# Hash experts' down projection as three half-precision products, and the engines' order lists searched anew

## The reference

```python
x = x + _L0_attn_ref(_layernorm(x), L0_attn_Wqkv, L0_attn_Wo)
x = x + _L0_xattn_ref(_layernorm(x), ctx_2048)
x = x + _L0_ffn_ref(_layernorm(x), ...)               # 16 routed experts and a shared one
x = x + _L1_attn_ref(_layernorm(x), ...)              # ternary weights
x = x + _L1_xattn_ref(_layernorm(x), tokens, ctx_2048, ctx_2048, ctx_2048)
x = x + _L1_ffn_ref(_layernorm(x), ...)               # ternary weights

# _L1_xattn_ref
for e in range(4):
    g = silu(einsum('bsd,fd->bsf', hidden, Wg[e]))
    u = einsum('bsd,fd->bsf', hidden, Wu[e])
    y = einsum('bsf,df->bsd', g * u, Wd[e])
    out = where(expert_ids == e, y, out)
```

## Time and profile before

| | before |
|---|---|
| median of 3 runs | 535.25 us (533.11 to 536.31) |
| profiled execution: device time | 534.2 us |
| profiled execution: span | 532.4 us |
| TensorE busy | 493.6 us, 93% |
| VectorE busy | 396.9 us, 75% |
| ScalarE busy | 345.2 us, 65% |
| GpSimd busy | 190.4 us, 36% |

### The profile page before, as it was taken

How to read it: one execution, slowest core, us unless ns; L and a number is a source line. 1 busy time by engine, 2 the same in 40 slices (tenths; PEclk the granted TensorE clock), 3 DMA queues, 4 the chain that set the end, 5 groups by cost and what they waited for, 6 DMA issues and landing times.

```text
span 532.4 us, 11834 instructions
## 1 busy us (share of the span) xinstructions
PE 493.6 (93%) x4694; PEld 362.3 (68%) x4721; DVE 396.9 (75%) x917; ACT 345.2 (65%) x601; POOL 190.4 (36%) x288
## 2 busy tenths in 40 slices
PE   5869887899999999999999999999999999999985
PEld 3424533567778788877887878777777676678654
DVE  2787997879677988548996587644876568689984
ACT  5666744766676236894269845588535874976796
POOL 3129986741340150330004072613052221032562
PEclk9987999899999999999999999999999999999999
DMA  8502443220000001000000020200000300000001
GB/s 290 216 0 63 149 162 114 71 81 1 1 3 1 2 10 71 1 2 2 1 1 2 1 80 3 81 1 1 1 1 2 120 1 1 1 2 2 0 27 55
DMA packets 5943, 21.66 MB, mean 41 GB/s; under 512 B 896, under 2 KB 3072, under 8 KB 5120
## 3 DMA queue, kind: packets, MB, share of 16 engines
q1 hardware_dynamic: 5888, 20.91, 11.6%
HBM read 19.86 MB, written 1.05 MB: 39 GB/s over the span
## 4 chain that ended last, share of the span: by engine, by line
PE 67%; DVE 16%; ACT 9%; issue 4%; POOL 3%; DMA 1%; ACTq 0%; DVEq 0%; POOLq 0%
PE ps L1072 24%; PE ps L1106 15%; PE ps L820 4%; DVE nmx L2524 3%; PE ps L951 3%; PE ps L844 2%; PE ps L880 2%; PE ps L1082 2%; PE ps L928 2%; PE ps L875 2%; PE ps L798 2%; PE ps L970 1%; PE ps L931 1%; DVE hl L2642 1%; PE ps L1152 1%
## 5 line engine op out<-in xcount | busy, mean ns | idle before, releaser
L2631 DVE TENSOR_TENSOR hs<-hs,ps 128x512 f32<-128x512 f32 (+1 forms) x68 | 45.2, 668 | 40.0 <-PE ps L1072 27.3
L1952 ACT ACTIVATE hs<-ps 128x512 f32<-128x512 f32 (+1 forms) x68 | 39.4, 581 | 51.1 <-PE ps L1072 42.7
L2524 DVE TENSOR_REDUCE nmx<-ps 128x2 f32<-128x512 f32 (+1 forms) x96 | 60.4, 681 | 7.2 <-PE ps L880 7.1
L556 POOL TENSOR_TENSOR ve<-mv,half 128x2 f32<-128x2 f32 x24 | 7.7, 322 | 149.0 <-DVE mv L2418 149.0
L1106 PE MATMUL ps<-w2h,hh 128*128 128x256 f16 x200 | 54.7, 274 | 0.7 <-DVE hl L2642 0.5
L1106 PE MATMUL ps<-w2h,hl 128*128 128x256 f16 x200 | 54.6, 273 | 0.0
L1106 PE MATMUL ps<-w2l,hh 128*128 128x256 f16 x200 | 54.6, 273 | 0.0
L1959 ACT ACTIVATE hh<-hs 128x512 f16<-128x512 f32 (+1 forms) x52 | 31.5, 611 | 34.5 <-DVE hs L2637 23.3
L2642 DVE TENSOR_TENSOR hl<-hs,hh 128x512 f16<-128x512 f32 (+1 forms) x52 | 40.1, 779 | 8.9 <-ACT hh L1959 8.6
L1911 ACT ACTIVATE pk<-ps 128x512 f32<-128x512 f32 x64 | 34.6, 597 | 12.1 <-PE ps L931 9.6
L1072 PE MATMUL ps<-yah,w1h 128*128 128x256 f16 x200 | 38.4, 274 | 1.9 <-DVE hs L2631 1.9
(11 more groups left out here) (249 smaller groups left out, 1338.5 us busy)
## 6 DMA issues: line engine op xcount, KB each, us to landing
stage<-in_w SPq DMA_DIRECT2D x12, 800.0 KB, 4.3
tstage<-in_tern SPq DMA_DIRECT2D x4, 1024.0 KB, 4.9
cs<-in_ctxT SPq DMA_DIRECT2D x1, 1024.0 KB, 9.4
cd<-in_ctxT SPq DMA_DIRECT2D x1, 1024.0 KB, 4.8
out_x<-xs SPq DMA_DIRECT2D x4, 256.0 KB, 2.2
sels<-in_sel SPq DMA_DIRECT2D x1, 800.0 KB, 9.8
w0s<-in_w SPq DMA_DIRECT2D x1, 768.0 KB, 7.0
xs<-in_x SPq DMA_DIRECT2D x1, 768.0 KB, 8.2
```

The lines of the kernel that those rows point to most:

```text
L1952: act.activation(hs[:, n % 3, 0:w], ps[:, gate_bank(n), 0:w], ACT.Silu).then_inc(e_sil.sem, 1)
L2524: dve.tensor_reduce(nmx[:, int(n % 3 > 0), first + par:first + 2 * heads:2], ps[:, max_bank(it, n) + par, :].rearrange("p (h k) -> p h k", ...
L2631: TT(hs[:, n % 3, 0:w], hs[:, n % 3, 0:w], ps[:, up_bank(n), 0:w], ALU.mult).then_inc(e_hb.sem, 1)
```

## The change

The hash pairs go the way of the mixture pairs: `inner_high` and `inner_low` for n = 52 to 67 too, and `down(n)` with `hh`, `hl` and the context's halves `ch` and `cl`. The fp32 tile `cd`, its DMA of 1 MB and its semaphore are gone. All four lists have a new order, and the numbers of `awake` matmuls are new (135 in `awake` calls of the list instead of 110).

```diff
-            sp.dma_start(cd[:, :, :, :], ctxT).then_inc(d_cd.sem, 16)
             def down(n):
                 kind, b, p = pair_of(n)
                 last = tiles_of(n) - 1
+                pe.wait_ge(e_lo.sem, n + 1)
                 if kind == "moe":
-                    pe.wait_ge(e_lo.sem, n + 1)
                     if p == 0 and b:
                         pe.wait_ge(xm_ok.sem, b)
                     bank, first, final = 1, p == 0, n + 1 == pairs_upto(kind, b)
-                    terms = [(hh[:, n % 2], w2h), (hh[:, n % 2], w2l), (hl[:, n % 2], w2h)]
+                    high, low = [t[:, 2 * p * D:2 * (p + 1) * D].rearrange("p (k d) -> p k d", d=D)
+                                 for t in (w2h, w2l)] if last else \
+                                [t[:, 2 * p * D:(2 * p + 1) * D].rearrange("p (k d) -> p k d", d=D) for t in (w2h, w2l)]
                 else:
-                    pe.wait_ge(e_hb.sem, n + 1)
-                    if n == ALL_MOE:
-                        pe.wait_ge(d_cd.sem, 16)
                     bank, first, final = gate_bank(n), True, True
-                    terms = [(hs[:, n % 3], None)]
+                    high, low = ch[:, p, :, :], cl[:, p, :, :]
+                terms = [(hh[:, n % 2], high), (hh[:, n % 2], low), (hl[:, n % 2], high)]
...
             def silu_of(n):
                 act.wait_ge(e_a.sem, n + 1)
                 if n >= 3:
-                    act.wait_ge(e_lo.sem if n - 3 < ALL_MOE else e_dn.sem, n - 2)
+                    act.wait_ge(e_lo.sem, n - 2)
...
             def inner_high(n):
-                act.wait_ge(e_hc.sem, n + 1)
+                act.wait_ge(e_hc.sem if n < ALL_MOE else e_hb.sem, n + 1)
```

Of the lists, the places that are spoken of below. GpSimd, start:

```diff
             split_lo(0)
-            context_split()
             split_lo(1)
             split_lo(2)
             split_lo(3)
             split_lo(4)
+            context_split()
+            rsqrt_ln('context', 0)
             split_lo(5)
-            rsqrt_ln('context', 0)
```

TensorE, start (`awake` after this: 30 up to `gate(0)` instead of 49):

```diff
             scores_max(0, 5)
+            awake(6, 3)
             project(1, 0)
+            awake(3, 14)
             maxima_turned(0)
             scores_exp(0, 0)
+            project(1, 1)
             scores_exp(0, 1)
-            project(1, 1)
...
-            awake(7, 10)
+            awake(7, 21)
             maxima_turned(1)
```

More of the change, by code:

```diff
@@ L724, in _ @@
             limited(4, 2)
+            rsqrt_ln('router', 3)
+            ternary(1)
             low_parts(5, 0)
             low_parts(5, 1)
-            ternary(1)
             limited(4, 3)
@@ L731, in _ @@
             ternary(2)
-            rsqrt_ln('tail', 0)
             limited(5, 0)
             limited(5, 1)
+            rsqrt_ln('tail', 0)
             rsqrt_ln('head', 6)
@@ L1350, in _ @@
             context_products(1)
+            scores_exp(2, 2)
             up(3)
@@ L1541, in _ @@
+            up(31)
+            project(5, 0)
+            logits(3)
+            spread(31)
+            gate(32)
+            up(32)
+            down(29)
+            scores_exp(4, 4)
+            project(5, 1)
+            spread(32)
+            gate(33)
             values(4, 0)
             values(4, 1)
-            gate(32)
-            up(32)
-            scores_exp(4, 4)
-            stack(5, 2)
-            down(30)
-            gate(33)
-            spread(32)
-            scores_exp(4, 5)
@@ L1551, in _ @@
-            stack(5, 3)
-            down(31)
-            up(33)
-            spread(33)
-            scores_max(5, 0)
-            gate(34)
-            up(34)
-            scores_max(5, 1)
-            spread(34)
-            back(4, 0)
-            gate(35)
-            up(35)
+            down(30)
+            up(33)
+            down(31)
+            spread(33)
+            back(4, 0)
+            gate(34)
+            scores_exp(4, 5)
+            up(34)
+            stack(5, 0)
+            down(32)
@@ L1563, in _ @@
+            spread(34)
+            stack(5, 1)
+            values(4, 2)
+            stack(5, 2)
+            values(4, 3)
+            scores_max(5, 0)
+            gate(35)
+            back(4, 1)
+            scores_max(5, 1)
+            up(35)
+            spread(35)
+            stack(5, 3)
             scores_max(5, 2)
-            down(32)
             gate(36)
-            spread(35)
-            values(4, 2)
-            values(4, 3)
+            down(33)
+            up(36)
             scores_max(5, 3)
-            up(36)
@@ L1614, in _ @@
             scores_exp(5, 4)
+            spread(42)
+            project(6, 0)
+            gate(43)
             up(43)
-            project(6, 0)
+            scores_exp(5, 5)
+            project(6, 1)
+            down(40)
+            down(41)
             back(5, 0)
+            spread(43)
             gate(44)
-            project(6, 1)
-            spread(43)
-            scores_exp(5, 5)
-            down(41)
-            down(42)
-            values(5, 2)
             up(44)
-            spread(44)
@@ L1639, in _ @@
             gate(46)
-            scores_max(6, 2)
             up(46)
-            down(44)
             scores_max(6, 3)
             spread(46)
+            back(5, 1)
             gate(47)
+            scores_max(6, 4)
             up(47)
-            scores_max(6, 4)
+            down(43)
+            scores_max(6, 5)
             spread(47)
+            gate(48)
+            down(44)
+            maxima_turned(6)
+            up(48)
             down(45)
-            scores_max(6, 5)
-            gate(48)
@@ L1689, in _ @@
             down(53)
+            back(6, 0)
+            down(54)
             values(6, 2)
             values(6, 3)
-            down(54)
-            back(6, 1)
             stack(7, 0)
             stack(7, 1)
-            gate(55)
+            back(6, 1)
+            gate(56)
+            scores_max(7, 0)
             stack(7, 2)
-            scores_max(7, 0)
-            gate(56)
             stack(7, 3)
@@ L1966, in sil @@
                     silu_of(first + k)
+                    if not is_mixture(it):
+                        inner_high(first + k)
             def high_left(it):
@@ L2664, in hb @@
                     times_up(first + k)
+                    if not is_mixture(it):
+                        inner_low(first + k)
             def hc(it, k):
@@ L2959, in _ @@
             moments_of('context', 3)
+            normalised('context', 3)
+            maximum(4, 4)
             times_up(24)
-            maximum(4, 4)
-            normalised('context', 3)
             times_share(24)
@@ L3117, in _ @@
             maximum(7, 4)
-            times_up(57)
             own_added(56)
             maximum(7, 5)
+            maxima_low(7)
+            times_up(57)
             times_up(58)
-            maxima_low(7)
+            experts_lo('hash', 2, 7)
+            inner_low(57)
+            times_up(59)
+            inner_low(58)
             moments_of('ffn', 0)
-            experts_lo('hash', 2, 7)
-            times_up(59)
             rounded_norm(0)
+            inner_low(59)
             own_added(57)
@@ L3132, in _ @@
             rounded_norm(1)
+            times_up(60)
             inner(0, 0)
-            times_up(60)
+            inner_low(60)
+            times_up(61)
+            inner(0, 1)
             normal(7, 1)
-            inner(0, 1)
             output_rounded(7)
+            own_added(60)
             inner(1, 0)
-            own_added(60)
             largest(0)
-            inner(1, 1)
-            times_up(61)
+            inner_low(61)
             times_up(62)
```

1021 lines of the change are left out of this document (515 added, 506 removed).

## The result

The changed kernel takes 543.48 us (median of 4 runs, 541.52 to 543.94) against 535.66 (533.11 to 536.31) for the kernel before in the same session: a ratio of 1.0152 with an interval of 1.0125 to 1.0179. It is slower, and lies above the forecast of 534.4 us and its range, 528.0 to 540.5.

What follows compares the result with a forecast made beforehand. TensorE was taken as the bound, with VectorE almost full too from 463 to 502 us. Terms -1.7 + 2.9 - 1.0 - 1.0 + 0 = -0.8 gave 533.4 us profiled, 534.4 median; range 528.0 to 540.5.

Steps and rivals of the forecast that it cites:

- The middle: 116 to 420 us: lists permuted without new work but two more ScalarE table switches; 0 taken, bounds -5 and +2.6.
- The second hash stage: normal(7, 0) to own_added(67): VectorE's work plus eight remainders, some rest and GpSimd meetings give 41.3 us, 2.9 longer.
- number of meetings: Second hash stage: eight remainders meet GpSimd's products 2.7 times by chance, 0.4 us each on average, 1.0 us in all.
- 1.1 us of rest: Second hash stage: VectorE's remaining idle time, against 4.2 us before, since its rests are mostly waits for a faster TensorE.
- Rival B: Second hash stage: remainders meet GpSimd's products by order, six of eight at 0.73 us; 539 us in total, chance 0.16.
- The first hash stage: 420 to 463 us: pairs 52 to 56 save 2.7 us on TensorE, 1.0 is given back; 1.7 us earlier.
- nothing arrives: First hash stage, 452.4 to 464.0 us: ScalarE paces it, so pairs 57 to 59's saving is lost and 1.0 given back.
- The tail: Last own additions to 528 us: the feed-forward's down(1) copies move ahead of it, 1.0 us shorter, bounds 0 and 2.
- TensorE's saving: All sixteen hash pairs' down products at 1.31 us each: 4.5 us saved before 463 us and 3.4 after, 7.9 in all.
- The start: Up to gate(0): keep-warm matmuls fill a slow-clock hole, against later exponentials; -1.0 us taken, bounds -4 and +4.
- gate(0) needs the last slice split: Start: gate(0), begun at 115.25 us, was taken to depend on the last slice split, at 113.80 us.
- rival C: Start: exponentials(1, ·) wait for GpSimd's rsqrt, so gate(0) comes 4 us later; 539.4 us in total, chance 0.10.

Runs made afterwards that it cites:

- e1: The changed kernel's new order with the edit undone (hash pairs in fp32, no remainders for them, cd and its transfer back): 542.32 us, ratio 1.0132.
- t1: The changed kernel with GpSimd's ternary scaling and clipping cut to 8 or 16 columns and the last operation only writing ones: 536.14 us, ratio 1.0050.
- t2: The kernel before with GpSimd's ternary scaling and clipping cut to 8 or 16 columns and the last operation only writing ones: 531.19 us, ratio 0.9954.
- p1: The changed kernel with GpSimd's products fh x lnwb replaced by three short memsets that only write fw: 539.55 us, ratio 1.0104.

## Why the prediction was wrong

**The middle** is the step that failed worst: "permuted without new work ... I take 0", with an upper bound of +2.6 that counted only ScalarE's two more table switches. It cost 5.7. I had priced meetings with GpSimd where the edit adds operations, with a row from the middle in hand, and did not ask whom GpSimd's ternary operations meet once the order is another. The bound should have come from those rows: GpSimd's dozen ternary operations are mostly 1.9 to 2.2 us long, and each may hold a VectorE operation that TensorE waits for. Three such holds, 1.57 at 199.76, 1.30 at 390.12 and 1.45 at 391.90 (each against its usual time), already make 4.3 us. The page of the Trainium skill that the prediction cites (SBUF — State Buffer, Who interferes with whom) has the rule that matters, exclusion for the whole instruction, and it names tensor_scalar among the operations that may take the shared ports although it has one input; the two-column rows at 390 and 392 agree: they took 1.47 and 1.68 us and ended 0.02 us behind GpSimd's.

**The second hash stage**, forecast +2.9, measured +6.3. By e1, 2.9 of the 6.3 are the order's, whose extra TensorE work in this stage the forecast did not look for, and 3.4 the edit's. On VectorE, which the forecast summed, the 5.0 us of the remainders was nearly right (8 x 0.68 = 5.5 where none meets), and so was their number of meetings, 2.7: it was three. The term that was sized wrong most is their price, 0.4 us each. Three cost 2.9 together, about 1.0 each, because a remainder that comes second waits for what is left of a 1.27 us product, and I had averaged over where it may begin. A fourth meeting, of y at 501.57, cost 1.0 more and was not in the sum. And "1.1 us of rest" was 2.2. That adds up to 4.5 over the forecast's terms, against 3.4 measured; 0.6 of the difference is a meeting of the kernel before that is gone (sf at 471.46, 0.74 us long instead of 0.17), the rest was not traced. Rival B had the mechanism, "slower by the port", with 0.16. It put the stage at the +6.3 that was measured, but by six meetings at 0.73 each, where three and that of y made it: the match is luck. Its total, 539, has nothing for the middle.

**The first hash stage**: -1.7 forecast, -1.6 measured, a match by luck. The edit gave 2.5 (e1 against the changed kernel) and the order took 0.9, which was no term of the sum. And the gain did not arrive where the forecast had it. It let pairs 52 to 56 save 2.7 us ahead of the last attention's exponentials, and said that of what 57 to 59 save "nothing arrives", with 1.0 given back. Measured from experts_added(3), the table load ahead of these exponentials begins at 39.8 us in e1 and 39.7 after. From there to normal(7, 0) it is 12.8 us in e1 and 10.3 after, because ScalarE, which paces this stretch, waits for TensorE in e1 and hardly after. First e1, then the changed kernel:

```profile
463.16 1.09 ACT L1916 ACTIVATE pk<-ps 128x512 f32<-128x512 f32 x2 [2.67 <-PE ps L931]
```

```profile
461.56 1.08 ACT L1910 ACTIVATE pk<-ps 128x512 f32<-128x512 f32 x2 [0.20 <-PE ps L928]
```

Which pairs' saving this is was not separated, and no run shows the 1.0 given back.

**The tail** came close: -1.0 and -1.3. e1 has 0.8 of it without the edit; that the copies of down(1) are the cause was not tried.

**TensorE's saving** was put at 7.9 us. The hash pairs do come at 1.31 to 1.43 us for 12, as two stretches of the chain show:

```profile
426.93 1.43 PE ps L1102 x12
...
487.59 2.62 PE ps L1102 x24
```

But the page has TensorE busy for 492.9 us against 497.9 in e1, which is 5.0. In the second hash stage TensorE was even busy for longer, 38.85 us instead of 38.00: the order brought in what the edit saved. This did not decide, since VectorE is the fullest engine there. (A slip without effect: the dropped load of cd had landed 6 us before its first reader, not 8.)

**The start** was -1.0 forecast and +0.8 measured. The mechanism came as described: the granted clock from 39.0 to 47.4 us went from 0.52 to 1.00, and project(1, 1) was 3 us earlier. But the step "gate(0) needs the last slice split" was wrong. The last slices were earlier than before:

```profile
109.77 3.65 POOL L573 TENSOR_TENSOR w3l<-stage,w3h 128x400 f16<-128x400 f32 x4
110.49 6.06 DVE L2539 TENSOR_REDUCE nmx<-ps 128x4 f32<-128x512 f32 x10
...
116.01 0.39 PE L1069 MATMUL ps<-yah,w1h 128*128 128x256 f16 x2 [0.32 <-DVE nmx L2539]
```

gate(0) began at 116.01, released by VectorE's maxima and not by GpSimd's slices, and the row of maxima began 0.8 us later than in the kernel before (110.49 against 109.72). There too gate(0) was released by the maxima, so the step was wrong for the old kernel already.

The 3 us of the early start are lost by 75 us, in the way that rival C described. normalised('context', 0), the y of these rows, now stands ahead of maxima_low(1) and waits 3.34 us for GpSimd, whose rsqrt_ln stands behind the context's split. It then takes 1.98 us beside a slice of GpSimd's, instead of 0.74. maxima_low(1) begins at 73.74 instead of 69.83, and TensorE stands for it:

```profile
71.72 1.98 DVE L2446 TENSOR_SCALAR y<-xs,mv,rstd 128x256 f32<-128x256 f32 x2 [3.34 <-POOL rstd L560]
74.71 0.39 PE L896 MATMUL ps<-idb,mtok 128*128 128x128 bf16 x2 [4.84 <-DVE mtok L2548]
...
72.00:86.00 14.00, 10.48 (x73) 4.69 (x76) 10.70 (x21) 7.71 (x16) 10.67 (x14) 0.51 0.34 117
```

In the kernel before, this matmul began at 71.41 after a wait of 1.44 us, and the granted clock was 1.00 from 72 to 86 us. The slow stretch was not removed by the change, it was moved, from 39 to 47 us to 72 to 86 us. C put the price at 4 us for gate(0); it was 0.8.

**Sum.** +0.8 + 5.7 - 1.6 + 6.3 - 1.3 = +9.8 between two profiled executions; the medians differ by 7.8, and the profiled execution of the changed kernel is the slowest of its four (543.94). The new order alone makes 9.0 of the 9.8 (e1's last ffn_added begins at 538.2, against 529.2 before and 539.0 after); on that order the edit adds 0.8, since its 3.4 in the second stage stand against 2.5 gained in the first. Of the 9.8, the meetings with GpSimd are 5.7 in the middle (t1, t2, net of the 2.7 that the old order pays too) and 3.5 in the second stage (p1); the order's other 2.9 there is made up by the first hash stage and the tail. The range missed because nothing was put down for meetings in the middle, and a meeting in the second stage was priced at the mean and not at the rest of GpSimd's instruction.

## What to carry to other kernels

When a change permutes an order that a search has found, the cost of the permutation is not zero even with no new work: list the long instructions of GpSimd (here 1.3 to 2.2 us) and ask which short VectorE operation on TensorE's path may start behind each of them. Here those at risk had all their inputs in SBUF, and a one-input tensor_scalar was among them. Price such a meeting at up to the whole remaining GpSimd instruction. Where order can't keep them apart, cut the long instruction where nobody waits for its end (the ternary weights, -0.4% on the kernel before), and leave it whole where somebody does (the products in the tail, +0.8 us). And when a wait ahead of a slow stretch of TensorE's clock is filled, look whether the stretch has only moved.

## What the runs showed of the hardware that was not expected

- A VectorE TENSOR_SCALAR on two columns took 1.47 and 1.68 us instead of 0.17 and 0.23 beside GpSimd operations of 1.9 us. It has one tile as input (and a per-partition scalar in the second case), and still ended only behind GpSimd's instruction. Not every overlap does this: sf at 284.43 took its 0.17 us inside a short GpSimd operation on two columns (283.95 to 284.64).
- GpSimd's write alone may hold it up too. In t1 the last ternary operation is a memset, and the same sf runs beside it; the memset ends at 386.22, sf at 386.25, after 0.36 instead of 0.17 us. It is one row, so this is a hint and not shown.

```profile
384.42 1.80 POOL L615 MEMSET wt<- 128x2048 f16 x1
385.89 0.36 DVE L2516 TENSOR_SCALAR sf<-am 128x2 f32<-128x2 f32 x1
```

- VectorE's operation gets through between two GpSimd instructions that stand back to back: with pieces of 0.68 us the same two operations took 0.55 and 0.17 us longer than alone.
- Cutting an operation into four costs GpSimd about the same whatever its width: 2048 columns took 1.97 us whole and 2.70 in four pieces (+0.7); a product of 512 columns 1.27 whole and 4 x 0.48 = 1.9 in four (+0.6). In share it is little on the wide one and much on the narrow one.
